# Two tail tiles per pair: subtracting the rounding grid on VectorE for one, on TensorE for the other

## The reference, cut to what matters

```python
def _quant_e4m3(t):
    scale = jnp.maximum(jnp.max(jnp.abs(t)) / 448.0, 1e-12)
    return (t.astype(jnp.float32) / scale).astype(jnp.float8_e4m3fn), scale

x = x + jnp.tanh(g_xattn[0]) * experts(_layernorm(x), ids, ctx)
w_fp8, w_scale = _quant_e4m3(weight)
x_fp8, x_scale = _quant_e4m3(_layernorm(x))
y = ((x_fp8 @ w_fp8.T) * (x_scale * w_scale)).astype(jnp.bfloat16)
x = x + jnp.tanh(g_ffn[0]) * y
```

## Time and profile before

| what | us |
|---|---|
| median of three runs | 205.53 |
| profiled execution, its own time | 204.08 |
| its span, first to last instruction | 202.2 |
| VectorE busy | 154.5 (76%) |
| TensorE matmul busy | 147.7 (73%) |
| ScalarE busy | 116.7 (58%) |
| GpSimd busy | 86.5 (43%) |

### The profile page before, as it was taken

How to read it: one execution, slowest core, us unless ns; L and a number is a source line. 1 busy time by engine, 2 the same in 40 slices (tenths; PEclk the granted TensorE clock), 3 DMA queues, 4 the chain that set the end, 5 groups by cost and what they waited for, 6 DMA issues and landing times.

```text
span 202.2 us, 3155 instructions
## 1 busy us (share of the span) xinstructions
PE 147.7 (73%) x759; PEld 73.7 (36%) x764; DVE 154.5 (76%) x348; ACT 116.7 (58%) x178; POOL 86.5 (43%) x120
## 2 busy tenths in 40 slices
PE   0232949798999999999989999999951285566700
PEld 0101425243555455555544454455420133233200
DVE  2886799879746999987988876556687899998720
ACT  2455596887455755688956562433222987666510
POOL 7167888230334323444467854211111014556670
PEclk9999999999999999999999999999996559999975
DMA  2837998200000000000000000000000002132341
GB/s 49 333 96 199 355 406 269 64 2 0 3 0 0 2 3 0 0 3 0 2 0 0 0 0 0 5 0 0 2 0 0 3 0 83 72 156 104 157 194 66
DMA packets 5646, 13.28 MB, mean 66 GB/s; under 512 B 1024, under 2 KB 1536, under 8 KB 5632
## 3 DMA queue, kind: packets, MB, share of 16 engines
q0 software_dynamic: 2560, 8.39, 11.4%
q1 hardware_dynamic: 2784, 4.73, 6.7%
q10 hardware_dynamic: 288, 0.00, 0.1%
HBM read 8.92 MB, written 4.19 MB: 65 GB/s over the span
## 4 chain that ended last, share of the span: by engine, by line
PE 36%; DVE 29%; ACT 12%; issue 11%; POOL 8%; DMA 1%; DVEq 1%; POOLq 0%
PE four_ps L437 9%; PE four_ps L429 9%; PE four_ps L442 9%; DVE w_hi L1007 3%; PE four_ps L469 3%; DVE hT_hi L1015 3%; POOL z L353 3%; POOL x L322 3%; PE four_ps L543 2%; DVE x L1019 2%; DVE w_lo L792 2%; ACT sg L592 2%; ACT y L671 2%; ACT w L583 2%; DVE bn L800 2%
## 5 line engine op out<-in xcount | busy, mean ns | idle before, releaser
L345 POOL DMA_INDIRECT out<-x,token_of x16 | 19.3, 1208 | 25.4 <-DVE x L1019 23.0
L353 POOL TENSOR_TENSOR z<-az,sg 128x512 f32<-128x512 f32 x15 | 19.0, 1267 | 25.6 <-ACT az L594 17.2
L340 POOL TENSOR_TENSOR rstd<-var,minus_half 128x1 f32<-128x1 f32 x16 | 8.8, 549 | 47.7 <-DVE var L856 47.7
L601 ACT ACTIVATE zT_hi<-four_ps 128x512 f16<-128x512 f32 x19 | 11.3, 595 | 21.5 <-PE four_ps L469 21.5
L592 ACT ACTIVATE sg<-four_ps,job_inv_a 128x512 f32<-128x512 f32 x19 | 13.0, 685 | 17.3 <-PE four_ps L442 15.9
L429 PE MATMUL four_ps<-w_hi,hT_hi 128*128 x76 | 21.4, 393 | 1.4 <-ACT w_hi L570 1.2
L842 DVE SCALAR_TENSOR_TENSOR x<-four_ps,job_mul,x 128x512 f32 x19 | 14.2, 749 | 9.8 <-PE four_ps L442 9.5
L322 POOL DMA_INDIRECT x<-in_x,token_of x16 | 17.4, 1087 | 7.0 <-issue 4.2
L429 PE MATMUL four_ps<-w_hi,zT_hi 128*128 x76 | 19.5, 379 | 0.8 <-ACT zT_hi L601 0.8
L437 PE MATMUL four_ps<-w_lo,zT_hi 128*128 x76 | 19.5, 379 | 0.0
L442 PE MATMUL four_ps<-w_hi,zT_lo 128*128 x76 | 19.5, 379 | 0.0
(11 more groups left out here) (147 smaller groups left out, 301.6 us busy)
## 6 DMA issues: line engine op xcount, KB each, us to landing
w<-in_ctx_t SPq DMA_DIRECT2D x4, 1024.0 KB, 9.5
wf<-in_wf_t SPq DMA_DIRECT2D x1, 512.0 KB, 16.4
x<-in_x,token_of POOLq DMA_INDIRECT x16, 5.9
out<-x,token_of POOLq DMA_INDIRECT x16, 2.7
g_s<-in_g_x ACTq DMA_DIRECT2D x1, 0.5 KB, 2.8
ids_s<-in_ids SPq DMA_DIRECT2D x1, 8.0 KB, 2.6
g_s<-in_g_f ACTq DMA_DIRECT2D x1, 0.5 KB, 6.4
```

The costliest lines, as they stand in the source:

```text
L345: pool.indirect_dma_start(out, bass.IndirectOffsetOnAxis(ap=token_of[:, i:i + 1], axis=0), block_of(x1, i), None, bounds_check=T - 1).then ...
L353: pool.tensor_tensor(z[:, :], az[:, :], sg[:, :], ALU.mult).then_inc(z_done, 1)
```

## The change

For each pair of tiles (groups 2 to 7), `rounded(g)` on VectorE computes `vt - vm` for the first tile alone. For the second tile TensorE computes it while it transposes: it multiplies the four blocks of `vm` (bf16) with minus the identity, and adds to that, in the same PSUM bank, the four blocks of `vt` (fp32) times the identity (fp32). The first tile's `q8` is transposed by ordinary matmuls with the identity, and so are the four single tiles. The transposed groups now stand in PSUM as fp32, in four banks (`q_ps`, one per tile) that the 16 tiles take in turn. GpSimd makes the extra constant `minus_ident` in the kernel's first microseconds. TensorE's `transposed(g)` waits for `vt_done` before the second tile's matmuls and for `q8_done` before the first tile's; `grid(g)` now waits for `qT_done` of the group that used its place before, since TensorE reads `vm` too.

```diff
+        minus_ident = sb("minus_ident", [P, P], BF16)
...
-        qT_ps = [n_ps[:, :].bitcast(BF16), r_ps[:, :].bitcast(BF16), c_ps[:, :].bitcast(BF16)]
-        NQ = len(qT_ps)
+        q_ps = psum("q_ps", [P, 4 * D], F32)
+        r_ps, c_ps, n_ps, m_ps = [q_ps[:, n * D:(n + 1) * D] for n in range(4)]
...
+        def split(g):
+            tiles = list(tiles_of(g))
+            return (tiles[:1], tiles[1:])
...
             pool.tensor_copy(ident_bf[:, :], ident[:, :]).then_inc(pool_const, 1)
+            pool.tensor_scalar(minus_ident[:, :], ident[:, :], -1.0, None, ALU.mult).then_inc(pool_const, 1)
...
-            def transpose_q(g):
+            def q_block(i, k):
+                return q_ps[:, i % 4 * D + k * P:i % 4 * D + (k + 1) * P]
+
+            def transposed(g):
+                by_dve, by_pe = split(g)
+                if reused(g, 4):
+                    pe.wait_ge(qT_copied, reused(g, 4))
+                pe.wait_ge(vt_done, g + 1)
+                for i in by_pe:
+                    for k in range(K):
+                        pe.matmul(q_block(i, k), vm[:, i % NB, k * P:(k + 1) * P], minus_ident[:, :],
+                                  start=(k == 0), stop=False)
+                    for k in range(K):
+                        pe.matmul(q_block(i, k), vt[:, i % NB, k * P:(k + 1) * P], ident[:, :],
+                                  start=False, stop=(k == K - 1))
                 pe.wait_ge(q8_done, g + 1)
-                if g >= NQ:
-                    pe.wait_ge(qT_copied, g - NQ + 1)
-                for n, i in enumerate(tiles_of(g)):
+                for i in by_dve:
                     for k in range(K):
-                        mm = pe.transpose(qT_ps[g % NQ][:, n * D + k * P:n * D + (k + 1) * P],
-                                          q8[:, i % NB, k * P:(k + 1) * P], ident_bf[:, :])
+                        mm = pe.matmul(q_block(i, k), q8[:, i % NB, k * P:(k + 1) * P], ident_bf[:, :],
+                                       start=(k == 0), stop=(k == K - 1))
                 mm.then_inc(qT_done, 1)
...
-                act.activation(ring(qT, g, NF), qT_ps[g % NQ][:, 0:n * D].rearrange("p (b d) -> p b d", d=D), ACT.Copy)\
+                act.activation(ring(qT, g, NF), ring(q_ps[:, :].rearrange("p (b d) -> p b d", d=D), g, 4), ACT.Copy)\
                     .then_inc(qT_copied, 1)
...
                 if reused(g, NB):
-                    dve.wait_ge(q8_done, reused(g, NB))
+                    dve.wait_ge(qT_done, reused(g, NB))
                 dve.tensor_scalar(ring(vm, g, NB), ring(v, g, NB), 1.5 * 2.0 ** -6, 2.0 ** 20, ALU.max, ALU.mult)\
...
                 dve.wait_ge(vt_done, g + 1)
-                if reused(g, NB):
-                    dve.wait_ge(qT_done, reused(g, NB))
-                dve.tensor_tensor(ring(q8, g, NB), ring(vt, g, NB), ring(vm, g, NB), ALU.subtract).then_inc(q8_done, 1)
+                i = split(g)[0][0]
+                dve.tensor_tensor(q8[:, i % NB, :], vt[:, i % NB, :], vm[:, i % NB, :], ALU.subtract).then_inc(q8_done, 1)
```

More of the change, by code:

```diff
@@ L520, in _ @@
             pe.matmul(m_ps[:, P:2 * P], ones_f[:, :], diag[:, :], start=True, stop=True).then_inc(xmax_done, 1)
-            def transpose_q(g):
+            def q_block(i, k):
[12 more added lines that the diff above has]
+                                  start=False, stop=(k == K - 1))
                 pe.wait_ge(q8_done, g + 1)
-                if g >= NQ:
-                    pe.wait_ge(qT_copied, g - NQ + 1)
-                for n, i in enumerate(tiles_of(g)):
+                for i in by_dve:
                     for k in range(K):
-                        mm = pe.transpose(qT_ps[g % NQ][:, n * D + k * P:n * D + (k + 1) * P],
-                                          q8[:, i % NB, k * P:(k + 1) * P], ident_bf[:, :])
+                        mm = pe.matmul(q_block(i, k), q8[:, i % NB, k * P:(k + 1) * P], ident_bf[:, :],
+                                       start=(k == 0), stop=(k == K - 1))
                 mm.then_inc(qT_done, 1)
-            pe.wait_ge(pool_const, 13)
+            pe.wait_ge(pool_const, 14)
             pe.wait_ge(wfq_done, K)
-            transpose_q(0)
+            transposed(0)
             for g in range(GROUPS):
                 if g + 1 < GROUPS:
-                    transpose_q(g + 1)
+                    transposed(g + 1)
                 pe.wait_ge(qT_copied, g + 1)
@@ L662, in copy_qT @@
                     act.wait_ge(f_done, reused(g, NF))
-                n = len(tiles_of(g))
-                act.activation(ring(qT, g, NF), qT_ps[g % NQ][:, 0:n * D].rearrange("p (b d) -> p b d", d=D), ACT.Copy)\
+                act.activation(ring(qT, g, NF), ring(q_ps[:, :].rearrange("p (b d) -> p b d", d=D), g, 4), ACT.Copy)\
                     .then_inc(qT_copied, 1)
```

## The result

The changed kernel runs in 203.5 us (median of four runs, 203.18 to 204.04), beside 205.84 us for the kernel before (205.48 to 206.47): a ratio of 0.989 with a 95% interval of 0.9853 to 0.9926. A second set gave 203.45 beside 206.45, 0.9844 (0.9819 to 0.9868). So it is 2.3 to 3.0 us faster; the forecast was 0.8. Medians and ranges are over all timed runs; the ratios leave out single runs more than 1.5% above the fastest of their kernel.

The account below looks back on a forecast made before the run. VectorE was taken to bound most of the tail, with waits for TensorE and ScalarE. Finish of group 6 coming 0.82 us earlier took the profiled 204.08 to 203.26 us and the median 205.53 to 204.7, range 203.7 to 206.3.

Parts of the forecast that it names:

- the sum: Tail's step times added up: the profiled execution goes from 204.08 to 203.26 us, 0.82 us gained.
- The 1.45 us: Distance of the timed median above the profiled execution of the kernel before; the same 0.82 us gain was put on the median.
- the clock comes back earlier: Rival, chance 0.18: TensorE's full clock in the tail from 163.4 us instead of 167.0, 1.52 us gained, 204.0 us.
- product(1): TensorE's product of group 1, early in the tail: begins at 165.96 us instead of 164.87, 1.09 us late.
- F(6): Start of group 6's finish on VectorE, ahead of the last stores: 186.37 us instead of 187.19, 0.82 us earlier.
- finish(1): VectorE's finish of group 1, early in the tail: begins at 168.87 us instead of 167.78, waiting for ScalarE.
- L: Time from one group's shifted moment until the previous group's finish may begin: 5.71 us, 0.40 shorter than 6.11.
- the fp32 record: One of two records per fp32 matmul on TensorE, eight per pair for `vt`: 0.11 us each at full clock.
- the hand-over from VectorE: Delay between VectorE's `vt` being ready and TensorE beginning the pair's matmuls: 0.04 us.
- The slower rival: Chance 0.17: fp32 weight loads on TensorE are not hidden, 0.21 us per record, 2.4 us later, 207.9 us.
- No gain: Rival, chance 0.18: TensorE's new matmuls take 0.02 to 0.03 us more per record, VectorE only waits more, 205.5 us.
- W(0): Moment of group 0's shifted step on VectorE, at the tail's start; `minus_ident` on GpSimd was to cost nothing.

Follow-up runs that it names:

- e13: The kernel before, unchanged, profiled in a single execution: 205.47 us.
- e14: The kernel before, unchanged, profiled in another single execution: 206.56 us.
- e15: The kernel before, unchanged, profiled in a third single execution: 206.55 us.
- e1: The kernel before, unchanged, run again: median 205.76 us (203.97 to 207.70).
- e5: The kernel before plus four dummy matmuls of 512 columns after the product of each group 2 to 7: 204.05 us.
- e9: The kernel before with VectorE subtracting for the first tile of each pair only, the second tile's rounded values left out: 203.30 us.
- e3: The kernel before plus 36 dummy matmuls in TensorE's idle time between the layers: 204.49 us.
- e4: The changed kernel plus 36 dummy matmuls in TensorE's idle time between the layers: 202.60 us.
- e12: The changed kernel plus 36 dummy matmuls between the layers and five after the first transposes, none after the products: 202.47 us.
- e7: The changed kernel plus dummy matmuls: 36 between the layers, five after the first transposes, two after the products of groups 1 to 7: 202.51 us.
- e10: e6 with VectorE subtracting for the first tile of each pair only, the second tile's rounded values left out: 201.31 us.
- e2: The changed kernel, unchanged, run again: median 203.45 us (203.15 to 204.00).
- e8: The changed kernel with VectorE subtracting for both tiles of a pair; ordinary matmuls for transposes and fp32 in PSUM stay: 206.56 us.
- e6: The kernel before plus dummy matmuls: 36 between the layers, five after the first transposes, four after every product up to group 7: 203.26 us.
- e11: e7 without the four fp32 matmuls of `vt` per pair, whose values are left out of the second tile: 200.94 us.

## Why the prediction was wrong

**The step that failed is the last one of the sum:** "The median of the runs lies 1.45 us above it; I put the same 0.82 on the median." The 1.45 us were taken as a constant that the change carries along. They were the clock: in e13, e14 and e15 the kernel before goes through one or two stretches of its rounds of pairs at 1.2 GHz, and the execution that the rows come from had none. The low mean clocks of most of its other runs (0.922 to 0.938 in e1) say the same, though a mean clock alone doesn't show where the clock was lost: two runs of e1 at 0.947 took 205.38 and 205.54 us. With the clock held in both, before and after are 203.26 and 202.51; left to itself, 205.8 to 206.5 and 203.5. So of the 2.3 to 3.0 us some 0.75 are the work that the sum had counted. The other 1.6 to 2.2 are what the kernel before loses and the changed kernel mostly keeps, by the clock for the most part: in the second set some 0.2 of it lies outside the spans (2.05 us of a run in the median before, 1.83 after), and no row here explains that.

**How it keeps it.** By the work that the change adds to TensorE. Load alone brings 1.15 to 1.9 us (e5). VectorE's saving alone doesn't: the one profile of e9 loses the clock. With the same 36 matmuls in front, the kernel before loses the clock among its pairs (e3, from 176.0) and the changed one doesn't (e4, e12). From 175 to 180 us TensorE works for 4.66 us in the changed kernel, where it had 2.50 before. The price fits: the added work costs 202.51 - 201.31 = 1.2 us where the clock is held (e7, e10), and 0.15 where it isn't (e2, e9), as it would if it gave most of its price back by the clock; the runs of e9 spread so far that the 0.15 is loose.

That the changed kernel never loses the clock in the tail isn't shown: its two profiles (203.22 and 204.00 us) show it full from 165.4 us on at the latest, but three of its ten runs, at 203.69 to 203.78 us, have a mean clock of 0.945 or 0.946, and none of them was profiled. Why the clock falls in one run of the same program and not in the next stays open.

**The rival "the clock comes back earlier" was half right.** In the changed profile it did, at 164.7 instead of 167.0, and product(1) began at 165.47 (165.96 forecast). That the change brought it isn't shown: e5, whose TensorE does until then what it does in the kernel before, has the rise at 164.7 too. Beyond that, the rival asked for one rise, and the earlier trace rows was read as showing that the clock then stays full. It showed that for one execution.

**The terms.** By its own rows the sum held: own time 203.22 against 203.26, F(6) 186.34 against 186.37. That it came so close is luck, since two errors met in it. The earlier clock gave about half a microsecond at finish(1), and L is 5.89 where 5.71 was said: the fp32 record is 0.119, not 0.11 (0.07 us in all), and the hand-over from VectorE 0.14, not 0.04, which e8 shows to come from the new transposing and not from fp32. The slower rival fell: eight records in a row, weight loads and all, keep 0.119 us, so the loads are hidden behind the matmuls. The rule of the Trainium skill cited for it ("TensorE: Matmul & The Clock Gate", Part 3), that a load overlaps running matmuls only on other rows of the array, doesn't hold for this sequence. "No gain" fell too. That VectorE's half subtraction lasts 0.69 us, that the copies read fp32 at no price (1.02 us as before), that `minus_ident` costs no more than 0.1 us (W(0) 158.11 beside 158.00), and that the last store follows F(6) by the same time (9.28 us after, 9.23 before) was right.

## What to carry to other kernels

Before a sum is made from a trace, hold the profiled execution against the timed runs: where it lies below all of them, its rows show an exception, and the difference is itself something that a change can move. Where TensorE works with gaps, read the granted clock over several executions: work added to TensorE, real or dummy, can pay as much as work saved elsewhere (2.6 us for dummy matmuls in e6, 1.95 for VectorE's saving with the clock held), and a change is best priced twice, with the clock held by dummy work and with it left alone.

## What the runs showed of the hardware that was not expected

- Dummy matmuls alone took the kernel before from 205.9 to 203.26 us and its runs' spread from 2.6 us or more to 0.05.
- A full clock at the tail's beginning doesn't last by itself: in e3 it was full from 150 us on and fell at 176.0, in e14 it rose at 171.2 and fell at 178.0, both times while TensorE went on working round by round, with gaps.
- Such a stretch costs a round 1.1 us (finish(3) to finish(4) in e14: 5.06 against 3.99), though VectorE is the busiest engine, since finish waits for the product.
- GpSimd's indirect stores can show spans up to 1.97 us without idle time, as in the changed kernel, and still not bound the end (e11).
- The clock can be lost while TensorE is busy with the first layer too: from 39.1 to 42.5 us in e2, from 30.1 to 33.5 in e13, and not at all there in e14.
- TensorE's ordinary 128x128 matmuls began 0.14 us after VectorE's end in e8, the transposes 0.05 us after it in the kernel before.
